# Reciprocal roots as element-wise powers on GpSimd, in eight sublayers on one core

## The reference, cut to what matters

```python
def _layernorm(x, axis=-1, eps=1e-05):
    m = jnp.mean(x, axis=axis, keepdims=True)
    v = jnp.var(x, axis=axis, keepdims=True)
    return (x - m) / jnp.sqrt(v + eps)

x = x + mamba(_layernorm(x));        x = x + local(_layernorm(x))
x = x + dense_attn(_layernorm(x));   x = x + local(_layernorm(x))
x = x + linear_attn(_layernorm(x));  x = x + fp4_ffn(_layernorm(x))
x = x + head_attn(_layernorm(x));    x = x + fp4_ffn(_layernorm(x))
```

```python
for i in range(DEPTH):
    x = attn_layer(shift_tokens(x), Wqkv[i], q_scale[i], k_scale[i], Wo[i]) + x
    x = ffn_layer(shift_tokens(x), ln_g[i], ln_b[i], W1[i], b1[i], W2[i], b2[i]) + x

# attn_layer: q, k, v = split(x @ Wqkv) in heads
def l2norm(t):
    return t / jnp.maximum(jnp.linalg.norm(t, axis=-1, keepdims=True), 1e-12)
q = l2norm(q) * qs;  k = l2norm(k) * ksc      # then rotary tables, local attention, @ Wo
# ffn_layer:
xn = (x - mu) / jnp.sqrt(var + 1e-05) * g + bln
a, gate = jnp.split(xn @ W1 + b1, 2, -1)
return a * gelu(gate) @ W2 + b2
```

## Time and profile before

| | |
|---|---|
| median of 3 runs | 4342.93 us (4341.33 to 4343.28) |
| profiled execution, from its first to its last instruction | 4339.8 us |
| median less that span | 3.1 us |
| busy: TensorE, its weight load | 3995.2 us (92%), 2655.5 us (61%) |
| busy: VectorE, ScalarE, GpSimd | 3715.0 us (86%), 3380.3 us (78%), 3380.2 us (78%) |
| mean granted TensorE clock | 0.957 of full speed |

### The profile page before, as it was taken

The page is one execution under the profiler, slowest core; times in us unless marked ns, Lnnn a source line. Parts: engine busy times, 40 slices in busy tenths (PEclk is TensorE's granted clock), DMA queues, the critical chain, the costliest instruction groups (busy, mean ns, idle before and its releaser), DMA issues. The chain is left out here.

```text
span 4339.8 us, 130231 instructions
## 1 busy us (share of the span) xinstructions
PE 3995.2 (92%) x46283; PEld 2655.5 (61%) x46283; DVE 3715.0 (86%) x12505; ACT 3380.3 (78%) x10657; POOL 3380.2 (78%) x4196
## 2 busy tenths in 40 slices
PE   6888799999999999999767999999999999996686
PEld 2333357767767767766553677767776776763464
DVE  6999789999999999999476999999999999974646
ACT  5888489999999999999414999999999999983122
POOL 3999698888888888888296888888888888861313
PEclk7999899999999999999897999999999999997887
DMA  1000101111111111111002111111111111100000
GB/s 28 1 1 1 46 24 31 41 31 36 41 27 49 31 34 44 26 34 27 15 1 53 31 27 41 36 41 31 36 41 27 51 29 29 37 24 3 6 3 10
DMA packets 78571, 122.04 MB, mean 28 GB/s; under 512 B 26024, under 2 KB 47204, under 8 KB 77924
## 3 DMA queue, kind: packets, MB, share of 16 engines
q1 hardware_dynamic: 77924, 113.71, 10.3%
HBM read 35.56 MB, written 1.05 MB: 8 GB/s over the span
## 5 line engine op out<-in xcount | busy, mean ns | idle before, releaser
L1095 POOL TENSOR_TENSOR local_qk<-local_qk,local_rb 128x512 f32<-128x512 f32 x768 | 975.7, 1271 | 224.2 <-DVE local_rb L1485 210.1
L1365 ACT ACTIVATE local_pr<-local_tb,local_nmax 128x96 f32<-128x96 f32 x3072 | 995.0, 362 | 68.7 <-DVE local_nmax L1501 67.1
L1191 PE MATMUL local_pj<-local_wqkv,local_xs 128*128 128x512 f32 x1536 | 808.4, 619 | 31.8 <-DVE local_rb L1485 17.8
L1101 POOL TENSOR_TENSOR local_qk<-local_qk,local_rinv 128x512 f32<-128x512 f32 x768 | 786.6, 1045 | 7.5
L1501 DVE CUSTOM_DVE_ANT_0 local_tb<-local_tb,local_mask 128x96 f32<-128x96 f32 x3072 | 689.2, 290 | 46.5 <-PE local_tb L1213 43.7
L1365 ACT ACTIVATION_READ_ACCUMULATOR local_pr<-local_tb,local_nmax 128x1 f32 x3072 | 703.3, 229 | 0.0
L1117 POOL TENSOR_TENSOR local_pr<-local_pr,local_rsum 128x384 f32<-128x384 f32 x768 | 622.4, 826 | 36.5 <-DVE local_rsum L1507 36.5
L1482 DVE TENSOR_TENSOR local_qk<-local_pj,local_rope 128x512 f32<-128x512 f32 x768 | 523.6, 682 | 62.8 <-ACT local_sq L1348 44.1
L1348 ACT ACTIVATE local_sq<-local_pj 128x512 f32<-128x512 f32 x768 | 462.2, 627 | 123.3 <-PE local_pj L1191 119.0
L1485 DVE TENSOR_TENSOR local_rb<-local_pj,local_rope 128x512 f32<-128x512 f32 x768 | 523.2, 681 | 2.8 <-POOL local_qk L1095 2.8
L1492 DVE TENSOR_REDUCE local_ss<-local_sq 128x8 f32<-128x512 f32 x768 | 512.0, 678 | 2.6 <-ACT local_sq L1348 0.8
(11 more groups left out here) (425 smaller groups left out, 7954.8 us busy)
## 6 DMA issues: line engine op xcount, KB each, us to landing
local_v<-local_v SPq DMA_DIRECT2D x288, 256.0 KB, 3.9
local_wqkv<-L_ffn_Wqkv_dram SPq DMA_DIRECT2D x72, 256.0 KB, 4.7
local_wo<-L_ffn_Wo_dram SPq DMA_DIRECT2D x12, 512.0 KB, 4.0
local_w<-L_ffn_W_dram SPq DMA_DIRECT2D x12, 341.0 KB, 4.8
mamba_parts<-mamba_in_low SPq DMA_DIRECT2D x24, 64.0 KB, 2.0
local_w<-L_ffn_W_dram SPq DMA_DIRECT2D x12, 128.0 KB
y_dram<-store_xtok SPq DMA_DIRECT2D x4, 256.0 KB, 2.9
local_oT<-rope_dram SPq DMA_DIRECT2D x2, 256.0 KB, 2.7
```

The costliest lines, as they stand in the source:

```text
L1095: nc.gpsimd.tensor_tensor(qk[:, u, :], qk[:, u, :], rb[:, u % 2, :], ALU.add).then_inc(s["summed"], 1)
L1101: nc.gpsimd.tensor_tensor(heads8(qk[:, u, :]), heads8(qk[:, u, :]), r, ALU.mult).then_inc(s["scaled"], 1)
L1191: nc.tensor.matmul(bank[:, :], xs[:, par, u // 4 * P:(u // 4 + 1) * P], wqkv[:, dep % 2, u % 4 * BANK:(u % 4 + 1) * BANK], start=True, sto ...
L1365: ins = nc.scalar.activation(pr[:, (NU * c + k) % PR_RING, i, WIN:WIN + KW], scores[:, i * KW:(i + 1) * KW], ACT.Exp, scale=-1.0, bias=nma ...
```

## The change

GpSimd raises the clamped sums, the variances of the eight normalisations and the variances of the FFN to the power -0.5, with one `tensor_tensor` instruction each and a constant tile `minus_half` as the second operand. The Newton code, its tiles and its steps in the orders of GpSimd and VectorE go away. In the normalisation the power stands behind `beside_pool` in GpSimd's stream; in the pipeline the deviation's power stands behind `add_parts(0, 3)`.

```diff
@@ constants
+        self.minus_half = root.sb("minus_half", [P, P // 2])
...
+            nc.gpsimd.memset(net.minus_half[:, :], -0.5)
@@ normalise
-            for r in root:
-                nc.gpsimd.memset(r[:, :], 0.0).then_inc(cleared, 1)
+            nc.gpsimd.memset(root[:, :], 0.0).then_inc(cleared, 1)
             for sem in net.past:
                 pool.sem_clear(sem)
             if beside_pool:
                 beside_pool(pool)
+            pool.wait_ge(cleared, 1)
+            pool.wait_ge(with_eps, 1)
+            nc.gpsimd.tensor_tensor(by_tile(root[:, :]), var[:, :, :], view(net.minus_half[:, 0:1], [[NT, NC], [1, NT]]), ALU.pow).then_inc(rooted, 1)
...
-            pe.wait_ge(roots, 1 + ROOT_STEPS)
-            nc.tensor.transpose(p_rootT, root[1][:, :], net.ident[:, :]).then_inc(turned, 1)
+            pe.wait_ge(rooted, 1)
+            nc.tensor.transpose(p_rootT, root[:, :], net.ident[:, :]).then_inc(turned, 1)
...
-            nc.vector.tensor_scalar(var[:, :, :], by_tile(p_var), LN_EPS, None, ALU.add).then_inc(roots, 1)
-            dve.wait_ge(cleared, 2)
-            dve.wait_ge(roots, 1)
-            inverse_root(nc, dve, roots, 1, var[:, :, :], [by_tile(r[:, :]) for r in root], [t[:, :, :] for t in tmp])
+            nc.vector.tensor_scalar(var[:, :, :], by_tile(p_var), LN_EPS, None, ALU.add).then_inc(with_eps, 1)
@@ local_transformer, GpSimd
-                    nc.gpsimd.tensor_scalar(x, ss[:, par, :], 1e-24, None, ALU.max).then_inc(s["root_steps"], 1)
+                    nc.gpsimd.tensor_scalar(ssc[:, :], ss[:, par, :], 1e-24, None, ALU.max).then_inc(s["root_steps"], 1)
                 else:
                     pool.wait_ge(s["root_steps"], ROOT_ALL * a + step)
-                    pool_root_step(nc, step - 1, x, y, t).then_inc(s["root_steps"], 1)
+                    nc.gpsimd.tensor_tensor(rinv[:, :], ssc[:, :], net.minus_half[:, :], ALU.pow).then_inc(s["root_steps"], 1)
+
+            def std(e, par, _):
+                pool.wait_ge(s["var_in"], e + 1)
+                need(pool, s["diag_ready"], e)
+                nc.gpsimd.tensor_tensor(deviation[:, :], var[:, :], net.minus_half[:, 0:2], ALU.pow).then_inc(s["std_ready"], 1)
...
                 run(add_parts, 0, 3)
+                run(std, 3, 0)
                 run(scale, 1, 6)
...
                 run(root, 0, 0)
                 run(root, 0, 1)
-                run(root, 0, 2)
...
-                run(root, 0, 13)
@@ ScalarE
-                act.wait_ge(s["std_steps"], STD_STEPS * e + STD_STEPS)
+                act.wait_ge(s["std_ready"], e + 1)
...
-                    ins = nc.scalar.activation(diag[:, t, :], net.ident[:, :], ACT.Copy, scale=newton[:, 1, t, 1:2])
+                    ins = nc.scalar.activation(diag[:, t, :], net.ident[:, :], ACT.Copy, scale=deviation[:, t:t + 1])
@@ VectorE
-                need(dve, s["diag_ready"], e)
-                nc.vector.tensor_scalar(var[:, :], fb[:, L:L + 2], LN_EPS, None, ALU.add)
-                nc.vector.tensor_scalar(newton[:, :, :, 3], view(fb[:, L:L + 2], [[0, 2], [1, 2]]), LN_EPS, -0.5,
-                                        ALU.add, ALU.mult).then_inc(s["var_in"], 1)
-            def std(e, par, step):
...
+                need(dve, s["std_ready"], e)
+                nc.vector.tensor_scalar(var[:, :], fb[:, L:L + 2], LN_EPS, None, ALU.add).then_inc(s["var_in"], 1)
...
                 run(add_eps, 4, 0)
-                run(std, 4, 0)
...
-                run(std, 4, 9)
```

More of the change, by code:

```diff
@@ L176, in _ @@
             sp.wait_ge(stored, 64)
[L180 to L224, removed]
 def warm(nc, net, bank, count):
@@ L247, in normalise @@
         var = m.sb("var", [P, NC, NT])
-        root = [m.sb(f"root{i}", [P, P]) for i in range(2)]
-        tmp = [m.sb(f"tmp{i}", [P, NC, NT]) for i in range(2)]
+        root = m.sb("root", [P, P])
         rootT = m.sb("rootT", [P, P])
@@ L253, in normalise @@
         p_var, p_rootT, p_idle = p_bc[:, NC - 1, 0:P], p_bc[:, NC - 2, 0:P], p_bc[:, 0, :]
-        cleared, centred, squared, summed, roots, turned, copied, spread = (
-            net.sem(f"{tag}_ln_{n}") for n in ("cleared", "centred", "squared", "summed", "roots", "turned", "copied", "spread"))
+        cleared, centred, squared, summed, with_eps, rooted, turned, copied, spread = (
+            net.sem(f"{tag}_ln_{n}") for n in ("cleared", "centred", "squared", "summed", "with_eps", "rooted", "turned", "copied", "spread"))
         x = net.xT[:, :, :].rearrange("p b l -> p (b l)")
@@ L828 @@
 PT_RING = 2
-POOL_STEPS = 1 + 3 * 4
-STD_STEPS = 1 + 3 * 3
+ROOT_ALL = 2
 V_BLOCK = (3, 0, 2, 1)
@@ L919, in local_transformer @@
         xs2 = m.sb("xs2", [P, L])
-        newton = m.sb("newton", [P, 2, 2, 7])
+        deviation = m.sb("deviation", [P, 2])
         EARLY_ROPES = 3
@@ L954, in prepare_margins @@
             nc.vector.memset(xs2[C // 2:C, 0:1], 0.0)
-            nc.vector.memset(newton[:, :, :, 6], 1.5)
             nc.vector.memset(v[0:QB, :, 3, :, :], 0.0)
@@ L966, in local_transformer @@
         ssc = m.sb("ssc", [P, 2 * 2 * HEADS])
-        root0 = m.sb("root0", [P, 2 * 2 * HEADS])
         rinv = m.sb("rinv", [P, 2 * 2 * HEADS])
-        rt = [m.sb(f"rt{i}", [P, 2 * 2 * HEADS]) for i in range(2)]
         rb = m.sb("rb", [P, 2, BANK])
@@ L995, in local_transformer @@
                  "root_steps scaled var_in probs_turned probs_copied qk_turned qk_copied scored maxed exped weighted "
-                 "pv_ready sum_inv o_copied wo_ready z1_ready xs2_ready centred squared2 var_ready std_steps diag_ready spread "
+                 "pv_ready sum_inv o_copied wo_ready z1_ready xs2_ready centred squared2 var_ready std_ready diag_ready spread "
                  "xn0_ready xn_ready up_ready gelu_ready g_ready down_ready z_ready").split()
@@ L1037, in couple @@
             return kk // 2, kk % 2
-        ROOT_ALL = 1 + POOL_STEPS
         @block.sync
@@ L1103, in root @@
             def root(a, par, step):
-                x, y, t = ssc[:, :], (root0[:, :], rinv[:, :]), [r[:, :] for r in rt]
                 if step == 0:
@@ L1530, in add_eps @@
                 dve.wait_ge(s["var_ready"], e + 1)
-                need(dve, s["diag_ready"], e)
-                nc.vector.tensor_scalar(var[:, :], fb[:, L:L + 2], LN_EPS, None, ALU.add)
-                nc.vector.tensor_scalar(newton[:, :, :, 3], view(fb[:, L:L + 2], [[0, 2], [1, 2]]), LN_EPS, -0.5,
-                                        ALU.add, ALU.mult).then_inc(s["var_in"], 1)
-            def std(e, par, step):
[L1538 to L1541, removed]
-                    ins = nc.vector.tensor_scalar(newton[:, 0, :, 1:3].bitcast(U32), view(var[:, :], [[1, 2], [0, 2]]).bitcast(U32), -0.5, SEED,
-                                                  ALU.mult, ALU.add)
-                else:
-                    dve.wait_ge(s["std_steps"], STD_STEPS * e + step)
-                    if part == 0:
-                        ins = nc.vector.tensor_reduce(old[:, :, 5], old[:, :, 1:4], AX.X, ALU.mult)
-                    elif part == 1:
-                        ins = nc.vector.tensor_reduce(old[:, :, 0], old[:, :, 5:7], AX.X, ALU.add)
-                    else:
-                        ins = nc.vector.tensor_reduce(new, view(old[:, 0, 0:2], [[7, 2], [0, 2], [1, 2]]), AX.X, ALU.mult)
-                ins.then_inc(s["std_steps"], 1)
+                need(dve, s["std_ready"], e)
+                nc.vector.tensor_scalar(var[:, :], fb[:, L:L + 2], LN_EPS, None, ALU.add).then_inc(s["var_in"], 1)
             def affine(e, par, _):
@@ L1591, in iteration @@
                 run(add_eps, 4, 0)
-                run(std, 4, 0)
-                run(std, 4, 1)
-                run(std, 4, 2)
-                run(std, 4, 3)
-                run(std, 4, 4)
-                run(std, 4, 5)
-                run(std, 4, 6)
-                run(std, 4, 7)
-                run(std, 4, 8)
                 run(recip, 2, 0)
-                run(std, 4, 9)
                 run(rotate, 1, 4)
```

## The result

| | before | after |
|---|---|---|
| median of 4 runs each | 4342.13 us (4340.14 to 4343.28) | 4943.90 us (4940.99 to 4944.31) |
| ratio, 95% interval | | 1.1388 (1.1372 to 1.1404) |
| profiled execution, span | 4339.8 us | 4942.2 us |
| mean granted TensorE clock | 0.957 | 0.915 |

The time is 601.8 us longer, or 6.27 us for each of the 96 sequences. The forecast was 4335.2 us with a range of 4326 to 4640, so the result lies 304 us above the range.

The account below looks back on a forecast made before the run. TensorE was taken to bound the long stretches. Fill -4.0, drain -5.9 and normalisations +2.2 sum to -7.7 us on the 4339.8 us span, 4332.1; with 3.1 for the median, 4335.2 us, range 4326 to 4640.

Parts of the forecast that it names:

- The bound of before: Long pipelined stretches are bound by TensorE, at 32.65 us a sequence for 96 sequences, with no idle time beside its starts.
- VectorE's relief: Deviations in the steady part: VectorE loses 2.3 us of steps, gaining nothing; rival that relief shows, 4325.6 us, chance 0.10.
- The price X: Length of GpSimd's 64-column power for the norms of queries and keys, taken as 2.2 us between 0.32 and 9.8.
- The cover of 6.5 us: How long the norms' power may last in the steady part before TensorE waits at the first turn of each sequence.
- The power is dearer than its cover: Rival at each sequence's first turn: every us of norms' power above 6.5 costs 96 times; chance 0.32.
- The upper bound of 4640: Top of the range, from a norms' power near 9.6 us costing +298 us; 0.17 chance left above.
- Fill: Start of both pipelines: TensorE's waits for the first scaled tile vanish, -4.0 us.
- Drain and deviations: Deviations cost 0 in the steady part; at both pipelines' ends TensorE's waits for the diagonal shorten, -5.9 us.
- Y: Length of GpSimd's 2-column power for the deviations, taken as 0.3 us; up to 1.9 us without moving ScalarE.
- Z: Length of GpSimd's 16-column power in a normalisation, taken as 0.7 us.
- Normalisations: Six of eight hidden by warming matmuls; the two ahead of the local transformers queue behind rope tables, +2.2 us together.
- The estimate of 6.4 us: Norms' 64-column power if it were thirty dependent steps of 4 cycles at 1.2 GHz; sum then about 4345 us.

Follow-up runs that it names:

- 32 columns: Changed kernel with the norms' power on only the first 32 of 64 columns, the others set to 1: 4353.74 us, ratio 1.0022 to before.
- 48 columns: Changed kernel with the norms' power on only 48 of its 64 columns, the others set to 1: 4532.69 us, ratio 1.0437 to before.
- the table of the five lengths: Periods of the changed kernel with the norms' power on 32, 40, 48 and 64 columns, and 64 with warming matmuls: 32.65, 33.05, 34.45, 38.93, 36.74 us.
- the warmed run: Changed kernel with 18 warming matmuls ahead of TensorE's wait for the first scaled tile: 4750.02 us, ratio 1.0944 to before.
- the four parts: Changed kernel with the norms' power split into four of 16 columns, each directly ahead of its two scalings: 4897.34 us, ratio 1.1278 to before.

## Why the prediction was wrong, point by point

**The bound of before.** Right. In every kernel whose power stays under 6.5 us the period is 32.65 us (deviations only, 32 columns), and VectorE's relief changed nothing there: its busy time in 200 us fell from 185.2 to 174.75 and TensorE's stayed at 200.

**The price X: the step that failed.** "Between ends so far apart I take X = 2.2" stands against 10.58 us measured, and the upper end, 9.8, was too low as well. No row gave the 2.2. It was picked between one product (0.32) and two Newton chains (9.8), near the 0.85 that the ratio of a reciprocal to a product on VectorE gives. The measured lengths lie on a line through the 708 ns of 2 columns, 2.91 us of 16, 5.46 of 32, 6.79 of 40, 8.05 of 48 and 10.58 of 64: 0.39 us and 0.159 us a column. A product costs 2.12 ns a column; the power is 75 times that. The reader can see that no row of before bears on this: a ratio between two instructions of one engine says nothing of an operation that neither is.

**The cover of 6.5 us.** Right, and it is the one number of the prediction that carries over: it was worked out from rows 2 and 3. The stands of TensorE are X less 6.45 us at 48 columns and X less 6.46 at 64, and the table of the five lengths follows it to 0.25 us wherever the clock holds.

**The rival and its price.** "The power is dearer than its cover" is what happened, with a chance of 0.32. Its formula gives 96 x 4.08 = 392 us, less than the 602 measured. The step left out was what TensorE does after it has stood, a term that the prediction put at nothing: 194 us, shown by the warmed run. With the fill, drain and normalisations as measured (+11.4, -5.1, +9.5, below) and 94 steady sequences of 4.08 us the sum is 4342.1 + 383.5 + 11.4 - 5.1 + 9.5 = 4741.4 us; the run with the clock kept up took 4750.0. The upper bound of 4640, which is the rival at X = 9.6, fell short for both reasons, the longer X and the clock.

**Also missed: GpSimd's sum.** The prediction weighed the place of the power and never its total. GpSimd had 173.5 x 32.65 / 200 = 28.3 us of work a sequence; exchanging 3.8 us of steps (their groups sum to 361.6 us over the 96 sequences of before) for 10.58 + 0.71 makes 35.8, as measured (35.9) and above the 32.65 that TensorE needs. With X as measured, that alone says slower, wherever the power stands, and it is the main reason why the four parts did not help: their 36.9 us of work are 4.3 of the 5.8 us a sequence.

**Fill.** The step was right and its sign followed X: instead of -4.0 us the first turn now stands 7.53 us:

```profile
541.39 1.12 PE L1190 MATMUL local_tb<-net_ident,local_qk 64*128 64x64 f32 x16 [7.53 <-POOL local_qk L1049]
```

Before, these two waits were 2.17 and 1.81 us, the 4.0 of the earlier trace rows. In the second pipeline it now stands 7.85 us, so the fill costs 5.4 + 6.0 = 11.4 us more.

**Drain and deviations.** Right but for the size of Y, 0.71 us for 0.3. By the formula of the prediction the chain becomes 0.08 + 0.71 = 0.79, 1.25 us shorter, so of the waits of 1.29 and 3.01 remain 0.04 and 1.76. The last wait of the changed kernel is

```profile
4522.79 1.23 PE L1218 MATMUL local_fb<-local_diag,net_ones 128*128 128x128 f32 x4 [1.75 <-ACT local_diag L1335]
```

The gain is 8.6 - 3.5 = 5.1 us; the run with the deviations alone took 7.4 less, and no row shows the other 2.3. Y stayed under its cover of 1.9, and in the changed kernel no diagonal was late in the steady part.

**Normalisations.** Z was 0.7 and is 2.9. So it outlasts the warming matmuls that were to hide it in five of those six. The sixth normalisation of the changed kernel, ahead of the first `fp4_ffn`:

```profile
4653.87 3.09 PE L186 MATMUL fp_ln_p_bc<-net_identb 128*128 128x512 bf16 x8
4654.04 0.18 DVE L276 TENSOR_SCALAR fp_ln_var<-fp_ln_p_bc 128x16 f32<-128x16 f32 x1 [7.48 <-PE fp_ln_p_bc L240]
...
4654.37 2.91 POOL L229 TENSOR_TENSOR fp_ln_root<-fp_ln_var,net_minus_half 128x16 f32<-128x16 f32 x1 [7.34 <-DVE fp_ln_var L276]
...
4657.33 0.48 PE L252 MATMUL fp_ln_p_bc<-net_ident,fp_ln_root 128*128 128x128 f32 x1 [0.37 <-POOL fp_ln_root L229]
```

TensorE waits 0.37 us here. In the run with the normalisations alone the six waits are 1.58, 0.68, 0.82, 0.23, 0 and 0.64, 3.95 us together. In the two ahead of the local transformers it stands 10.1 us for the power, where it stood 3.1 for VectorE's root: 7.0 more, near the 0.8 + Z + Z = 6.6 of the prediction's own sum. Together 10.9; measured 9.5.

**The estimate of 6.4 us, and the move of the small roots.** The price in the Trainium skill of 4 cycles for each dependent fp32 step (GPSIMD Engine Reference, section 7) gave an estimate of 6.4 us under the assumption of thirty steps. The measured 10.58 us decides; since no run shows the steps inside the instruction, it says that the assumed number of steps was too low or the rule too cheap, and not which. The Trainium skill also has elementwise work slower on GpSimd (GPSIMD Engine Reference, section 3), and the prediction took this to speak against moving the small roots. That is borne out for 16 columns, 2.91 us against VectorE's 2.1, and not for 2 columns, 0.71 against a chain of 2.04 (ten small steps that a single power replaces).

**The version that wins.** The deviations alone as powers: 4332.67 us, 0.9984 of before (0.9975 to 0.9993). It is faster than both kernels, by less than the 0.2% that I had called the bound of a measurement; eleven runs of it against twenty of before resolve it.

## What to carry to other kernels

Price a replaced chain by its number of columns. A chain of small instructions costs mostly its fixed parts, and the power costs by the element. Here it takes 0.39 us + 0.159 us a column: 2 columns take 0.71 us and replace 2.04, 64 columns take 10.58 and replace 4.76. An equal length is not the limit either: 32 columns take 5.46 us, longer than the 4.76 of the 64-column chain, and cost nothing in the steady part, because they stay under the cover. When an operation has no row in the trace, compare the cover (how late may it be?) and the engine's free time in a period (how much may it add?) first. Here they were 6.5 us and 4.3 us, and either is a question that one measurement of the operation would have answered.

When an engine ahead of TensorE becomes late, ask what the clock adds to the stand. In this kernel a stand of 1.6 us a sequence left the clock full and cost 1.8 us, and one of 4.1 us cost half as much again.

## What the runs showed of the hardware

A power of 128 x n values on GpSimd takes 0.39 us + 0.159 us x n, within 0.05 us over six lengths from 2 to 64 columns, and its length at 64 columns varies by 7 ns over a stretch of 44 of them.

A stand of 4.12 us left TensorE's granted clock at 1.00 during the stand itself and at 0.57 in the 4 us behind it, so the loss shows on matmuls that wait for nothing. 18 warming matmuls in the stand removed it, and 194 us of the time. A stand of 1.60 us in every sequence left the clock at 1.00.
